# Expert blocks of 256 rows in place of 128 in a routed feed-forward kernel

## The chip, the core and the metric

One NeuronCore of a Trainium2 chip runs the whole kernel in one launch. The metric is the device time of one execution in microseconds. The core has five engines that run their own instruction lists and meet at semaphores: TensorE (PE) multiplies matrices, VectorE (DVE) and ScalarE (ACT) work on tiles, GpSimd (POOL) does small tile work and issues the indirect DMAs, SyncE (SP) issues most plain DMAs. A semaphore is a counter: one instruction raises it when it ends, another waits until it has reached a value. Matrix products land in PSUM, eight banks of 512 f32 columns on 128 partitions; everything else on the chip lies in SBUF.

## The reference

The input x has 16 sequences of 256 tokens with 128 features: 4096 rows. Three residual steps follow each other:

```
x = x + 0.5 * ffn(layernorm(x))
x = x + attn(layernorm(x))
x = x + 0.5 * ffn(layernorm(x))

def ffn(x_):                                  # x_ is [4096, 128]
    idx = argmax(x_ @ router.T)               # one of 8 experts for each row
    h_e = silu(x_ @ gate[e].T) * (x_ @ up[e].T)          # 256 wide, e = idx of the row
    y   = h_e @ down[e].T
    ys  = silu(x_ @ w_gate_s.T) * (x_ @ w_up_s.T) @ w_down_s.T    # the shared expert, for all rows
    return y + ys
```

`attn` is a circular convolution, a decayed sum over the sequence and a circular correlation; the change doesn't touch it. Everything is computed in f32.

## The kernel before

**The two expert stages.** Each `ffn` sends every row to its expert through HBM. While the rows are normalised and routed, POOL scatters them, 128 rows with one indirect DMA (line 334, 32 of them in a stage), into a buffer `dispatched` that has a region for each expert. A row takes its token number along. Behind the last row of each expert a full block of pad rows is written (`send_pads`, lines 242 to 246), so that a block that is only partly filled reads pads. The experts' rows are then cut into blocks of `P` = 128 rows. Since each expert's last block may be partly filled, there are `NB` = 32 + 7 = 39 blocks at most. The instruction list always has 39; blocks beyond those really needed repeat the last one and write their result to a part of the result buffer that nobody reads. DVE works out small tables from the routing counts: which expert each block has, where its rows begin, where its results go (`block_experts` and `tables`, lines 687 to 720).

**One block** takes these steps. SP loads its 128 rows (line 289). PE transposes them (line 882), two blocks at a time into one bank, so that features lie on partitions, and ACT copies the pair to SBUF (line 479). ACT also copies the expert's gate and up weights into a ring of four (`copy_up`, line 463), and DVE the down weights (`copy_down`, line 728). PE multiplies: four products with a 128x128 weight tile held in the array and the block's 128 columns moved past it, two for gate and two for up, all into one bank (line 893). ACT takes silu of the gate half (line 485), DVE multiplies it with the up half (line 742). PE makes the down product: two products that add up, with the hidden tile held and 128 columns of weights moved (line 901). DVE copies the 128x128 result out (line 747), and POOL scatters it to the tokens' rows of `returned` with one indirect DMA (line 363). When all 39 scatters have landed, SP loads `returned` back in token order (line 293), and the rows are added to x.

**The order on each engine is written out by hand.** PE does for step b: gate and up of block b+1 (`gate_up_block`), down of block b-1 (`down_block`), and at every second step a pair of transposes for blocks b+3 and b+4 (lines 909 to 921). ACT does for step b: silu of b+1, the weight copy of b+3, and at every second step the copy of the next transposed pair (lines 487 to 497). DVE does: result of b-1 out, multiply of b+1, weight copy of b+2 (lines 749 to 757). POOL waits for the result of b, scatters it, and computes token rows for a pair of blocks at every second step (lines 367 to 372). An instruction that waits holds back all that stands behind it on its engine. POOL's scatters wait for nothing but their results, and nobody reuses what a scatter reads within the stage.

**Around the experts** PE, ACT and DVE also work through the shared expert in parts with 512 columns (lines 816, 824, 436, 580); some parts lie before the blocks and some behind them. Before the blocks, SP and ACT write the pads, SP waits until pads and dispatched rows have landed, and loads the blocks one after the other. POOL fills the tile of pad rows once, early in the first stage (line 395), between scatters and the small steps of the norm.

Of the kernel before, what the change touches and what calls it, by code (L numbers as in the profile page):

```python
# [14 lines left out]
E = 8  # L15
# [10 lines left out]
CAP = N + P  # L26
X_LOADS = ((0, 1), (1, 2), (2, 4), (4, G))
AHEAD = 3
NB = NT + E - 1
NBL = NB + 1  # L30
BU = 8
PAIRS = NBL // 2
LOADS = NBL // BU
WR = 4
AHEAD_UP = 3
AHEAD_DOWN = 2
DUMP = N + E * P
# [19 lines left out]
def build(nc, x_in, gu_in, dn_in, router_in, bind_in, unbind_in, gate_in, decay_in, out):  # L57
# [6 lines left out]
    with ExitStack() as ctx:  # L64
# [21 lines left out]
        pads = sb("pads", [P, E, ROW])  # L86
# [56 lines left out]
        xs = sb("xs", [P, NBL, ROW])  # L143
        token = sb("token", [P, NBL], I32)
        xsT = sb("xsT", [P, 2, 2, P])
        eg = sb("eg", [P, WR, H])
        eh = sb("eh", [P, WR, H])
        wgu = sb("wgu", [P, WR, 2 * H])
        wdn = sb("wdn", [P, WR, HH * C])
        ey = sb("ey", [P, NBL, C])  # L150
# [40 lines left out]
        blk_in = [sem(f"blk_in{b}") for b in range(NBL)]  # L191
# [19 lines left out]
        def by_tile(ap):  # L211
            return ap.rearrange("p (t e) -> p t e", t=TPG)

# [21 lines left out]
        def y_of(b):  # L235

            return bank[2 + b % 2][:, 0:C]
# [4 lines left out]
        def send_pads(eng, experts):  # L242

            for e in experts:
                row = eng.value_load(pad_row[0:1, e:e + 1], min_val=0, max_val=E * CAP - P)
                eng.dma_start(dispatched[bass.ds(row, P), :], pads[:, e, :]).then_inc(pad_sent, 16)
# [8 lines left out]
        def _(sp):  # L255
# [19 lines left out]
            def block_row(b):  # L275
                return sp.value_load(tab_row[0:1, b:b + 1], min_val=0, max_val=E * CAP - P)

            sp.wait_ge(table_const, N_TABLE_CONST)
            for f in range(2):
# [11 lines left out]
                sp.wait_ge(blk_out, 16 * NB * (f + 1))  # L291
# [7 lines left out]
        def _(pool):  # L299
# [52 lines left out]
            def experts(f):  # L352
                def tokens(pair):

                    pool.wait_ge(blk_turn, f * PAIRS + pair + 1)
                    two = slice(2 * pair, 2 * pair + 2)
                    nc.gpsimd.tensor_tensor(token[:, two], xs[:, two, C].bitcast(I32), to_replica[:, two],
                                            ALU.add).then_inc(blk_tok, 1)

                def send(b):  # L360
                    pool.wait_ge(blk_tok, f * PAIRS + b // 2 + 1)
# [7 lines left out]
                for b in range(NB):  # L369
                    if b % 2 == 0 and b + 2 < NBL:  # L370
                        tokens(b // 2 + 1)
# [24 lines left out]
            nc.gpsimd.iota(pads[:, :, C:C + 1].bitcast(I32), [[P, E], [0, 1]], base=N, channel_multiplier=1,  # L396
# [9 lines left out]
        def _(act):  # L406
# [52 lines left out]
            def copy_up(b):  # L459

                if b % BU == 0:
                    digits[0] = load_digits(act, b // BU)
                nc.scalar.activation(wgu[:, b % WR, :], tile(gu, expert_of(digits[0], b)),  # L463
                                     ACT.Copy).then_inc(blk_wgu, 1)
# [11 lines left out]
            def experts(f):  # L476
                def evac_pair(pair):
                    act.wait_ge(blk_turn, f * PAIRS + pair + 1)
                    nc.scalar.activation(xsT[:, pair % 2, :, :],  # L479
                                         bank[pair % 2][:, 0:2 * P].rearrange("p (s c) -> p s c", s=2),  # L480
                                         ACT.Copy).then_inc(blk_xT, 1)

                def silu(b):
                    act.wait_ge(blk_gu, f * NB + b + 1)
                    nc.scalar.activation(eg[:, b % WR, :], bank[4 + b % WR][:, 0:H], ACT.Silu).then_inc(blk_silu, 1)  # L485

                evac_pair(0)
                silu(0)
                for b in range(NB):
                    if b + 1 < NB:  # L490
                        silu(b + 1)
                    if b == 0:
                        evac_pair(1)
# [489 lines left out]
```

## Time and profile before

| | |
|---|---|
| time of the runs | 323.37, 328.67 and 329.10 us, median 328.67 us |
| profiled execution | 329.47 us, of which 327.7 us lie between the first and the last instruction (the span) |
| busy over the span | PE 262.4 us (80%), PE weight loads 213.1 (65%), DVE 185.5 (57%), POOL 185.2 (57%), ACT 160.3 (49%) |
| mean granted TensorE clock | 0.944 of full speed |
| scatters of results (line 363) | 78 in both stages, 77.5 us busy, mean 993 ns |
| gate and up products (line 893) | 624 steps, 85.8 us busy |
| down products (line 901) | 312 steps, 48.2 us busy |
| result copies (line 747) | 78, mean 290 ns, 64.0 us of idle DVE before them |

A product of two f32 tiles shows as two matrix steps in the trace, so that a block's four gate and up products are eight steps. The ends of matrix steps are modelled, their starts are recorded: the cost of a step in a row of steps is read from one start to the next. A line of the timeline merges instructions of one kind that follow each other; in brackets stands how long the engine was idle before, and whose end was taken to have released it. "remote" there means that no instruction was found that did.

### The profile page before, as it was taken

Reading aid. Unit: us, or ns where it says so; the run is one execution under the profiler, and the core shown is the slowest. Engines: PE = TensorE matmul, PEld = TensorE weight load, DVE = VectorE, ACT = ScalarE, POOL = GpSimd, SP = SyncE. Lnnn points to the kernel's source line nnn. Section 1 sums busy time; section 2 is a strip of 40 time slices with the busy share of each in tenths; the row PEclk is TensorE's granted clock in tenths of the full one; section 3 lists DMA queues with packets and bytes.
Section 4 is the critical chain, followed back from the end, with each engine's and each line's share of the span. In section 5 each row is a group of like instructions: output and inputs, shape, how many; then the busy total and the mean of one; then the engine's idle time right before and its main releaser. Section 6 shows DMA issues by size and latency. Waiting matters only on the chain.

```text
span 327.7 us, 6436 instructions
## 1 busy us (share of the span) xinstructions
PE 262.4 (80%) x1788; PEld 213.1 (65%) x1788; DVE 185.5 (57%) x722; ACT 160.3 (49%) x374; POOL 185.2 (57%) x268
## 2 busy tenths in 40 slices
PE   0898996498988898896499889976898969989750
PEld 0566664267987798864386657753598969989430
DVE  3448551574453545538999898727644525544362
ACT  3545431035664666523699668510456545656200
POOL 4488787321656665662447888774125566576500
PEclk9999999599999999999859979995999997999996
DMA  7941111132333331119000111111323333211189
GB/s 190 370 180 43 41 50 53 34 99 61 90 91 96 97 82 34 49 41 254 5 1 25 40 37 35 34 58 57 86 67 95 87 93 91 67 41 43 40 234 279
DMA packets 34996, 28.42 MB, mean 87 GB/s; under 512 B 4784, under 2 KB 31792, under 8 KB 34704
## 3 DMA queue, kind: packets, MB, share of 16 engines
q1 hardware_dynamic: 25328, 16.06, 17.5%
q0 software_dynamic: 4544, 9.45, 8.6%
q10 hardware_dynamic: 5088, 2.50, 2.6%
q8 instruction: 14, 0.23, 0.3%
q14 instruction: 22, 0.18, 0.2%
HBM read 15.37 MB, written 12.62 MB: 85 GB/s over the span
## 4 chain that ended last, share of the span: by engine, by line
PE 42%; POOL 11%; DVE 10%; another core or an unknown queue 10%; issue 8%; ACT 6%; DMA 6%; SPq 3%; POOLq 1%; ACTq 1%; DVEq 0%
PE bank L893 21%; PE bank L901 7%; POOL dispatched L334 5%; PE bank L816 4%; DMA ey<-returned 3%; PE bank L882 2%; ACT wgu L463 2%; PE bank L841 2%; PE bank L824 2%; POOL scale_f L323 2%; DVE xres L548 2%; DVE st_f L532 2%; PE bank L802 2%; ACT xsT L479 2%
## 5 line engine op out<-in xcount | busy, mean ns | idle before, releaser
L363 POOL DMA_INDIRECT returned<-ey,token x78 | 77.5, 993 | 52.7 <-DVE ey L747 35.7
L893 PE MATMUL bank<-xsT,wgu 128*128 128x128 f32 x624 | 85.8, 281 | 14.9 <-ACT xsT L479 9.6
L893 PEld LDWEIGHTS bank<-xsT,wgu 128*128 128x128 f32 x624 | 76.7, 194 | 19.6 <-ACT xsT L479 11.7
L334 POOL DMA_INDIRECT dispatched<-xn,slot x64 | 64.2, 1003 | 26.2 <-issue 17.2
L816 PE MATMUL bank<-xnT,gu 128*128 128x512 f32 x128 | 68.1, 662 | 1.2 <-issue 0.4
L747 DVE COPY ey<-bank 128x128 f32<-128x128 f32 x78 | 22.6, 290 | 64.0 <-PE bank L901 52.3
L485 ACT ACTIVATE eg<-bank 128x256 f32<-128x256 f32 x78 | 29.9, 383 | 47.3 <-PE bank L893 42.0
L436 ACT ACTIVATE sg<-bank 128x512 f32<-128x512 f32 x32 | 19.0, 593 | 69.1 <-PE bank L816 30.0
L463 ACT ACTIVATE wgu<-gu 128x512 f32 x78 | 48.4, 625 | 3.5 <-issue 3.4
L901 PE MATMUL bank<-wdn,eh 128*128 128x128 f32 x312 | 48.2, 278 | 1.8 <-DVE eh L742 1.5
L901 PEld LDWEIGHTS bank<-wdn,eh 128*128 128x128 f32 x312 | 41.5, 194 | 2.4 <-DVE eh L742 1.9
L816 PEld LDWEIGHTS bank<-xnT,gu 128*128 128x128 f32 x128 | 24.0, 207 | 21.5 <-issue 20.5
L824 PEld LDWEIGHTS bank<-dn,hs 128*128 128x128 f32 x256 | 31.0, 196 | 10.6 <-DVE hs L580 7.0
L824 PE MATMUL bank<-dn,hs 128*128 128x128 f32 x256 | 32.4, 281 | 4.9 <-DVE hs L580 4.0
L742 DVE TENSOR_TENSOR eh<-eg,bank 128x256 f32<-128x256 f32 x78 | 32.2, 412 | 5.7 <-ACT eg L485 4.6
L412 ACT ACTIVATE xn<-xres,shift_f,scale_f 128x128 f32<-128x128 f32 x64 | 26.3, 484 | 12.5 <-POOL shift_f L327 12.5
L580 DVE TENSOR_TENSOR hs<-sg,bank 128x512 f32<-128x512 f32 x32 | 21.9, 683 | 12.5 <-ACT sg L436 9.6
L728 DVE COPY wdn<-dn 128x256 f32 x78 | 23.4, 300 | 4.1 <-issue 4.1
L841 PEld LDWEIGHTS bank<-routerT,xnT 128*128 128x128 f32 x128 | 18.3, 213 | 9.5 <-issue 7.4
L323 POOL TENSOR_TENSOR scale_f<-var_f,minus_half 128x4 f32<-128x4 f32 x16 | 16.4, 1026 | 10.0 <-DVE minus_mean_f L543 9.7
L603 DVE TENSOR_REDUCE top<-bank 128x4 f32<-128x32 f32 x16 | 3.1, 192 | 30.7 <-remote 17.1
L841 PE MATMUL bank<-routerT,xnT 128*128 128x8 f32 x128 | 17.7, 265 | 2.8 <-ACT xnT L427 1.3
(96 smaller groups left out, 290.2 us busy)
## 6 DMA issues: line engine op xcount, KB each, us to landing
xs<-dispatched SPq DMA_DIRECT2D x80, 66.0 KB, 1.9
ey<-returned SPq DMA_DIRECT2D x16, 256.0 KB, 5.1
gu<-in_gu SPq DMA_DIRECT2D x1, 2048.0 KB
out<-xres ACTq DMA_DIRECT2D x8, 256.0 KB, 5.0
returned<-ey,token POOLq DMA_INDIRECT x78
dn<-in_dn SPq DMA_DIRECT2D x1, 1024.0 KB
dispatched<-xn,slot POOLq DMA_INDIRECT x64
dispatched<-pads SPq DMA_DIRECT2D x10, 66.0 KB
```

Source lines behind the costliest of these rows:

```text
L334: nc.gpsimd.indirect_dma_start(dispatched[:, :], bass.IndirectOffsetOnAxis(slot[:, i:i + 1], 0), xn[:, i, :], None, bounds_check=last_row) ...
L363: nc.gpsimd.indirect_dma_start(returned[:, :], bass.IndirectOffsetOnAxis(token[:, b:b + 1], 0), ey[:, b, :], None, bounds_check=last_back) ...
L412: nc.scalar.activation(dst[:, at * TPG + t, 0:C], xres[:, i, :], ACT.Identity, bias=shift[kind][:, i:i + 1], scale=scale[kind][:, i:i + 1] ...
L463: nc.scalar.activation(wgu[:, b % WR, :], tile(gu, expert_of(digits[0], b)), ACT.Copy).then_inc(blk_wgu, 1)
L485: nc.scalar.activation(eg[:, b % WR, :], bank[4 + b % WR][:, 0:H], ACT.Silu).then_inc(blk_silu, 1)
L728: nc.vector.tensor_copy(wdn[:, b % WR, :], tile(dn[:].rearrange("p e h c -> p e (h c)"), expert_of(digits[0], b)))
L742: nc.vector.tensor_tensor(eh[:, b % WR, :], eg[:, b % WR, :], bank[4 + b % WR][:, H:2 * H], ALU.mult).then_inc(blk_mul, 1)
L816: last = nc.tensor.matmul(ps[:], gu[:, SHARED, at:at + P], xnT[:, g, :], start=True, stop=True)
L824: last = nc.tensor.matmul(o_ps[:, t * C:(t + 1) * C], hs[:, n % 2, h, t * P:(t + 1) * P], dn[:, SHARED, h, :], start=(h == 0), stop=(h == ...
L841: last = nc.tensor.matmul(rt[:, t * E:(t + 1) * E], xnT[:, k, t * P:(t + 1) * P], routerT[:], start=True, stop=True)
L893: last = nc.tensor.matmul(bank[4 + b % WR][:, i * P:(i + 1) * P], wgu[:, b % WR, i * P:(i + 1) * P], xsT[:, b // 2 % 2, b % 2, :], start=T ...
L901: last = nc.tensor.matmul(y_of(b), eh[:, b % WR, h * P:(h + 1) * P], wdn[:, b % WR, h * C:(h + 1) * C], start=(h == 0), stop=(h == HH - 1))
```

## The change

Blocks have 256 rows (`BW` = 2 x 128). The number of blocks in the list falls from 39 to 16 + 7 = 23, that of 128-row halves rises from 39 to 46. Partition p of a loaded block holds rows 2p and 2p+1, so that each partition's load is one run of 1056 bytes in place of 528. Gate and up have a bank each, and each of the four weight tiles meets 256 columns. Silu and multiply work on 512 columns, the result copy on 256. The down products stay 128 columns wide, and there are four for a block. Two indirect DMAs of 128 rows send a block's results. Rings of transposed rows, hidden tiles and banks have two blocks; a gate product now waits for the multiply of two blocks before (`blk_mul`). The pads of each expert are 256 rows. The main parts of the diff:

```
+SUB = 2
+BW = SUB * P
+CAP = N + BW
-NB = NT + E - 1
+NB = N // BW + E - 1
+RING = 2
...
-        pads = sb("pads", [P, E, ROW])
+        pads = sb("pads", [P, E, SUB, ROW])
...
+        def gate_of(b):
+            return bank[4 + 2 * (b % RING)]
+        def up_of(b):
+            return bank[5 + 2 * (b % RING)]
+        def block_at(row):
+            return dispatched[bass.ds(row, BW), :].rearrange("(p s) c -> p s c", s=SUB)
...
 (SP)
-                for b in range(NBL):
+                for b in range(NB):
                     row = rows[b] if b < 2 else block_row(b)
-                    sp.dma_start(xs[:, b, :], dispatched[bass.ds(row, P), :]).then_inc(blk_in[b], 16)
+                    sp.dma_start(xs[:, b, :, :], block_at(row)).then_inc(blk_in[b], 16)
...
 (POOL)
+                    pool.wait_ge(blk_tok, f * NB + b + 1)
                     pool.wait_ge(blk_y, f * NB + b + 1)
-                    nc.gpsimd.indirect_dma_start(
-                        returned[:, :], bass.IndirectOffsetOnAxis(token[:, b:b + 1], 0),
-                        ey[:, b, :], None, bounds_check=last_back).then_inc(blk_out, 16)
+                    for t in range(SUB):
+                        nc.gpsimd.indirect_dma_start(
+                            returned[:, :], bass.IndirectOffsetOnAxis(token[:, b, t:t + 1], 0),
+                            ey[:, b * SUB + t, :], None, bounds_check=last_back).then_inc(blk_out, 16)
...
 (ACT)
+                evac_rows_of(0)
+                evac_rows_of(1)
                 silu(0)
+                evac_rows_of(2)
                 for b in range(NB):
                     if b + 1 < NB:
                         silu(b + 1)
                     if b + AHEAD_UP < NB:
                         copy_up(b + AHEAD_UP)
+                        evac_rows_of(b + AHEAD_UP)
...
 (DVE)
-                    nc.vector.tensor_copy(ey[:, b, :], y_of(b)).then_inc(blk_y, 1)
+                    nc.vector.tensor_copy(ey[:, b * SUB:(b + 1) * SUB, :],
+                                          y_of(b)[:, 0:SUB * C].rearrange("p (t c) -> p t c", t=SUB)).then_inc(blk_y, 1)
...
 (PE)
+                def turn_block(b):
+                    pe.wait_ge(blk_in[b], (f + 1) * 16)
+                    for t in range(SUB):
+                        last = nc.tensor.transpose(bank[b % RING][:, t * P:(t + 1) * P], xs[:, b, t, 0:C], ident[:])
                     last.then_inc(blk_turn, 1)
...
+                    pe.wait_ge(blk_xT, f * NB + b + 1)
+                    wait_pos(pe, blk_mul, f * NB + b - RING + 1 if b >= RING else 0)
+                    for ps, at in ((gate_of(b), 0), (up_of(b), H)):
+                        for h in range(HH):
+                            last = nc.tensor.matmul(ps[:, h * BW:(h + 1) * BW],
+                                                    wgu[:, b % WR, at + h * P:at + (h + 1) * P], xsT[:, b % RING, :],
+                                                    start=True, stop=True)
                     last.then_inc(blk_gu, 1)
...
+                    for t in range(SUB):
+                        for h in range(HH):
+                            last = nc.tensor.matmul(y_of(b)[:, t * C:(t + 1) * C],
+                                                    eh[:, b % RING, h, t * P:(t + 1) * P],
+                                                    wdn[:, b % WR, h * C:(h + 1) * C],
+                                                    start=(h == 0), stop=(h == HH - 1))
                     last.then_inc(blk_dn, 1)
...
+                turn_block(1)
                 gate_up_block(0)
+                turn_block(2)
                 for b in range(NB):
                     if b + 1 < NB:
                         gate_up_block(b + 1)
+                    if b > 0:
                         down_block(b - 1)
+                    if b + AHEAD_UP < NB:
+                        turn_block(b + AHEAD_UP)
                 down_block(NB - 1)
```

## Rows read from the trace of the kernel before

**Rows 1.** Stretches, both expert stages: us, PE, PEld, DVE, ACT, POOL busy, PEclk, DMA, GB/s
```profile
74.90:145.60 70.70, 63.13 (x513) 58.80 (x514) 32.46 (x116) 39.55 (x95) 42.55 (x58) 1.00 0.26 72
237.30:310.30 73.00, 64.64 (x514) 60.27 (x515) 33.27 (x117) 39.50 (x95) 42.66 (x58) 0.98 0.25 70
```
**Rows 2.** Timeline of PE: start, length (us), line, operation, shape, count [idle before]
```profile
74.98 2.02 PE L893 MATMUL bank<-xsT,wgu 128*128 128x128 f32 x16 [0.68 <-ACT xsT L479]
...
80.75 1.06 PE L893 MATMUL bank<-xsT,wgu 128*128 128x128 f32 x8
81.64 0.61 PE L901 MATMUL bank<-wdn,eh 128*128 128x128 f32 x4
82.09 0.38 PE L882 MATMUL bank<-ident,xs 128*128 128x128 f32 x2
82.31 1.06 PE L893 MATMUL bank<-xsT,wgu 128*128 128x128 f32 x8
...
142.76 3.70 PE L816 MATMUL bank<-xnT,gu 128*128 128x512 f32 x8 [0.38 <-issue]
```
**Rows 3.** Timeline of PE, the second stage's first products
```profile
237.37 2.05 PE L893 MATMUL bank<-xsT,wgu 128*128 128x128 f32 x16 [0.98 <-DVE xres L548]
```
**Rows 4.** Timeline of POOL, result scatters of the first stage, 39 in all
```profile
80.47 1.00 POOL L363 DMA_INDIRECT returned<-ey,token  x1 [2.97 <-DVE ey L747]
...
85.97 0.97 POOL L363 DMA_INDIRECT returned<-ey,token  x1 [1.59 <-DVE ey L747]
...
87.33 1.00 POOL L363 DMA_INDIRECT returned<-ey,token  x1 [0.16 <-issue]
88.64 0.97 POOL L363 DMA_INDIRECT returned<-ey,token  x1 [0.30 <-issue]
...
91.44 1.00 POOL L363 DMA_INDIRECT returned<-ey,token  x1 [1.61 <-DVE ey L747]
...
112.46 1.00 POOL L363 DMA_INDIRECT returned<-ey,token  x1 [0.73 <-issue]
113.76 0.97 POOL L363 DMA_INDIRECT returned<-ey,token  x1 [0.30 <-issue]
...
115.66 1.00 POOL L363 DMA_INDIRECT returned<-ey,token  x1 [0.71 <-issue]
...
144.63 0.97 POOL L363 DMA_INDIRECT returned<-ey,token  x1 [0.30 <-issue]
```
**Rows 5.** Timeline of POOL, first and last of 39 scatters of the second stage
```profile
242.89 1.00 POOL L363 DMA_INDIRECT returned<-ey,token  x1 [2.97 <-DVE ey L747]
...
309.31 0.97 POOL L363 DMA_INDIRECT returned<-ey,token  x1 [0.30 <-issue]
```
**Rows 6.** Timeline of ACT, silu of two blocks in the first stage
```profile
81.84 0.39 ACT L485 ACTIVATE eg<-bank 128x256 f32<-128x256 f32 x1 [0.44 <-PE bank L893]
...
88.86 0.38 ACT L485 ACTIVATE eg<-bank 128x256 f32<-128x256 f32 x1 [1.47 <-PE bank L893]
```
**Rows 7.** Timeline of PE around 87 us
```profile
86.65 1.16 PE L893 MATMUL bank<-xsT,wgu 128*128 128x128 f32 x8
87.65 0.61 PE L901 MATMUL bank<-wdn,eh 128*128 128x128 f32 x4
```
**Rows 8.** Timeline of DVE, a result copy
```profile
90.39 0.29 DVE L747 COPY ey<-bank 128x128 f32<-128x128 f32 x1 [2.37 <-PE bank L901]
```
**Rows 9.** Timeline of all engines around 270 us, second stage
```profile
267.87 1.00 POOL L363 DMA_INDIRECT returned<-ey,token  x1 [0.16 <-issue]
...
269.78 0.38 ACT L485 ACTIVATE eg<-bank 128x256 f32<-128x256 f32 x1 [3.28 <-remote]
...
270.73 2.08 PE L893 MATMUL bank<-xsT,wgu 128*128 128x128 f32 x8 [2.36 <-ACT wgu L463]
```
**Rows 10.** Timeline of POOL, the pad tile is filled
```profile
21.55 0.98 POOL L395 MEMSET pads<- 128x1056 f32 x1
```
**Rows 11.** Chain of waits ahead of the first stage: pads landing, after SP's last issue
```profile
69.77 1.65 DMA dispatched<-pads
```

More of the change, by code:

```diff
@@ L190, in build @@
         selfed, x2_done = sem("selfed"), sem("x2_done")
-        blk_in = [sem(f"blk_in{b}") for b in range(NBL)]
+        blk_in = [sem(f"blk_in{b}") for b in range(NB)]
         blk_out = sem("blk_out")
@@ L244, in send_pads @@
             for e in experts:
-                row = eng.value_load(pad_row[0:1, e:e + 1], min_val=0, max_val=E * CAP - P)
-                eng.dma_start(dispatched[bass.ds(row, P), :], pads[:, e, :]).then_inc(pad_sent, 16)
+                row = eng.value_load(pad_row[0:1, e:e + 1], min_val=0, max_val=E * CAP - BW)
+                eng.dma_start(block_at(row), pads[:, e, :, :]).then_inc(pad_sent, 16)
         def wait_pos(eng, s, value):
@@ L369, in experts @@
                 for b in range(NB):
-                    if b % 2 == 0 and b + 2 < NBL:
-                        tokens(b // 2 + 1)
+                    if b + 1 < NB:
+                        tokens(b + 1)
                     send(b)
@@ L877, in experts @@
             def experts(f):
-                def turn_pair(pair):
-                    for t in range(2):
-                        pe.wait_ge(blk_in[2 * pair + t], (f + 1) * 16)
-                        last = nc.tensor.transpose(bank[pair % 2][:, t * P:(t + 1) * P], xs[:, 2 * pair + t, 0:C],
-                                                   ident[:])
+                def turn_block(b):
+                    pe.wait_ge(blk_in[b], (f + 1) * 16)
+                    for t in range(SUB):
+                        last = nc.tensor.transpose(bank[b % RING][:, t * P:(t + 1) * P], xs[:, b, t, 0:C], ident[:])
@@ L884, in turn_pair @@
                     last.then_inc(blk_turn, 1)
                 def gate_up_block(b):
-                    if b % 2 == 0:
-                        pe.wait_ge(blk_xT, f * PAIRS + b // 2 + 1)
-                    if b % 2 or b < AHEAD_UP:
-                        pe.wait_ge(blk_wgu, f * NB + b + 1)
-                    for i in range(2 * HH):
-                        last = nc.tensor.matmul(bank[4 + b % WR][:, i * P:(i + 1) * P],
-                                                wgu[:, b % WR, i * P:(i + 1) * P], xsT[:, b // 2 % 2, b % 2, :],
-                                                start=True, stop=True)
+                    pe.wait_ge(blk_xT, f * NB + b + 1)
@@ L896, in gate_up_block @@
                     last.then_inc(blk_gu, 1)
                 def down_block(b):
-                    pe.wait_ge(blk_mul, f * NB + b + 1)
-                    for h in range(HH):
-                        last = nc.tensor.matmul(y_of(b), eh[:, b % WR, h * P:(h + 1) * P],
-                                                wdn[:, b % WR, h * C:(h + 1) * C],
-                                                start=(h == 0), stop=(h == HH - 1))
+                    if b + RING >= NB:
+                        pe.wait_ge(blk_mul, f * NB + b + 1)
```

74 lines of the change are left out of this document (32 added, 42 removed).

## The prediction

> **What bounds the kernel now.** I read the stretches first. Each expert stage, from its first product to the end of its last scatter, takes 70.6 us (74.98 to 144.63 + 0.97) and 72.9 us (237.37 to 309.31 + 0.97) [rows 1 to 5]; together that is 44% of the span, and nearly all of the change lies in it. PE is busy 63 of 71 us, at the full clock level in the first stage and 0.98 of it in the second; DVE and ACT are busy for about half [rows 1]. So it looks bound by PE.
>
> The timeline of PE says how much of that is needed. In an unbroken run the eight steps of a block's gate and up products start at 80.75 and the down steps at 81.64: 0.89 us, or 0.111 us a step. The transposes follow 0.45 us later, and a pair of them costs 0.22 us (82.09 to 82.31) [rows 2]. Thirty-nine blocks need 39 x (0.89 + 0.45) + 20 x 0.22 = 56.7 us. The stage takes 14 to 16 us more.
>
> The timeline of POOL shows what goes with the rest. The 39 scatters run from 80.47 to 145.60, 65.1 us, and in the second stage from 242.89 to 310.28, 67.4 us [rows 4, 5]: 1.67 and 1.73 us each, though one follows another after only 1.31 us (87.33 to 88.64) or, with a token step between, 1.36 us (85.97 to 87.33). They come in bursts: three from 85.97, the last ending at 89.61, then 1.83 us of nothing until 91.44 [rows 4]. What ends the pause is a result copy of DVE, which had waited 2.37 us for a down product and started at 90.39 [rows 8].
>
> That wait is the core of my reading. Where POOL had not yet scattered in a burst, silu starts at 81.84, 0.03 us behind the gate step's end at 81.81 [rows 2, 6]. In the burst, gate and up end at 87.81 and silu starts at 88.86, 1.05 us late; the down product behind them ends at 88.26 and its copy starts at 90.39, 2.1 us late and 0.8 us after the burst's end [rows 4, 6 to 8]. PE's starts show no gap there. So from about the second scatter of a burst on, **news of finished PE work reaches ACT and DVE late**, until POOL pauses. POOL pauses only when it lacks results, which is when DVE hasn't heard of a down product: the stage swings between the two. A longer burst holds longer: after one whose last scatter starts at 267.87, ACT had waited 3.28 us when it starts again at 269.78, PE has stood 2.36 us, and its next products take 2.08 us in place of 1.16 [rows 7, 9]: the lower of the clock's two levels, 1.2 GHz for 2.4.
>
> **The change, part by part** (for each stage, against 329.47 us for the profiled execution, 327.7 of it span; this execution is 0.8 us above the median).
>
> *PE.* A step of 512 columns costs (3.70 - 0.66) / 7 = 0.43 us from start to start, 0.66 being one step's own mean length, 3.9 times the 128-column one [rows 2]. A 256-column step is not in the trace: at least 0.111 us, at most two of 128, 0.223. On the line between the two widths it is 0.219, and I take that. Gate and up of a block: 8 x 0.219 = 1.75 us; four down products 0.89; two transposes 0.22; sum 2.86 us, for 23 blocks 65.8 us. That is 9 us **more** than before: 46 halves in place of 39, and little saved by wider steps.
>
> *ACT and DVE.* Fewer and longer instructions, 23 of a kind for 39. Their half-idle rows [rows 1] leave room for 46/39 of the columns; I cost this at nothing. If the cover were gone, the added columns would show, at most 7/39 of their busy time: 6 us of DVE, 7 of ACT. The result copy is the exception: it stands between a down product and POOL. One of 128 columns takes 0.29 us [rows 8], one of 256 between 0.29 and 0.58; I take 0.43, the middle.
>
> *Until the first scatter.* Before, 5.49 us from the first product (74.98 to 80.47) [rows 2, 4] and 5.52 in the second stage [rows 3, 5]. After: three gate and up groups, two turns and a down group, 3 x 1.75 + 2 x 0.22 + 0.89 = 6.58, the copy 0.43, and 0.76 for POOL to begin (the copy from 90.39 ends at 90.68, the scatter starts at 91.44 [rows 4, 8]): 7.77 us, **+2.26**.
>
> *The scatters.* Forty-six. Bounds: unbroken, POOL needs 2.67 us for two, 46/2 x 2.67 = 61.3 us, less than before; PE's 2.86 for a block gives nearly the same end. At the other end, bursts of one block: 1.31 + 0.97, then the pause of 1.83 + 0.14 for the longer copy, 4.25 us a block, 96 us. Between them, bursts of two blocks: 1.31 + 1.36 + 1.31 + 0.97 + 1.97 = 6.92, 3.46 a block. The nearest row is a burst of two scatters as it stands in the trace: 112.46, 113.76, then 115.66, **3.20 us for two** [rows 4]. I take that: three-scatter bursts by the sum give 5.47 / 3 = 1.82, and the stages average only 1.70, so sums of bursts come out some 7% high, and 3.46 less 7% is 3.2 too. 22 x 3.20 + 2.28 = 72.7 us, against 66.3 on average: **+6.4**.
>
> *The new waits.* Gate and up of block b+1 wait for the multiply of b-1; behind them on PE stand down b-1 and the turn of b+3, and ACT's copy of those rows waits for that turn. From the last news that ACT had, PE has down, turn, gate and up, down, turn to do: 0.89 + 0.22 + 1.75 + 0.89 + 0.22 = 3.97 us, about twice what it had (0.45 + 0.22 + 0.89 + 0.45 = 2.01). That shelters PE from a hold of 3 us, but not POOL, which still gets no results in it. So I add nothing here.
>
> *Ahead of the stage.* POOL's fill of the pads doubles, 0.98 us more [rows 10], with scatters queued behind it on POOL that run without a break: +1.0, once. Pads are twice the bytes; the last of them lands 1.65 us after its issue [rows 11], between nothing and another 1.65 more: +0.5 a stage. The first loads are longer too, in part under DVE's own end in the second stage [rows 3]; left in that 0.5. SP's queue gets 23 loads in place of 40. The tables on DVE get shorter; pads are later than tables, so nothing.
>
> *Sum.* 2 x (2.26 + 6.4 + 0.5) + 1.0 = 19.3 us: 348.8 us for the profiled execution, **348 us** for the median, slower by 5.9%.
>
> **Rivals.**
>
> *The holds go with something that the change cuts.* The loads of blocks share the stage with the scatters, and become fewer with longer runs; if the late news comes of them, PE's order sets the end: 65.8 less the two turns ahead of the first product 0.43, then 0.43 + 0.76 + 2.28, 68.8 us from first product to last scatter, against 71.8. 2 x (-3.0 + 0.5) + 1.0 = -4.0: about 325 us, not slower. For it: PE's doubled lead. Against it: the timing follows POOL's bursts, and POOL has only 2.86 - 2.67 = 0.19 us a block to make up pauses. It decides if pauses after bursts fall under some 0.2 us.
>
> *Holds grow with the longer burst.* Bursts of two blocks are the rule at 3.46: 22 x 3.46 + 2.28 = 78.4, 2 x (2.26 + 12.1 + 0.5) + 1.0 = +30.7: 359 us. For it: the longer burst with its stop and lower clock [rows 9]. Against: the 7%.
>
> *Weights set the step, not columns.* Then a 256-column step costs little more than 0.111 us, say 0.135: gate and up 1.08, a block 2.19 us, and POOL alone bounds the stage. First scatter after 3 x 1.08 + 2 x 0.22 + 0.89 + 0.43 + 0.76 = 5.76, +0.25; run 61.3 to 72.7; 320 to 343 us, 331 in the middle. Against it: 512 columns cost 3.9 times 128 [rows 2]. The Trainium skill (TensorE: Matmul & The Clock Gate, section Back-to-back issue gap) speaks for it: in a stream of weight loads and products a product of 128 columns comes every 81 ns and one of 512 every 131 ns, 1.6 times for four times the columns. By that rule an estimate for 256 columns is 1.2 times a 128-column step, which gives the 331 us; the trace disagrees, with 0.43 to 0.111.
>
> **How the numbers follow.** A measurement of this kernel can tell about 2%, 322 to 335 us. My forecast has 0.54 (340 to 353 us), longer holds 0.20 (353 to 364), holds gone 0.21 (321 to 332), weights 0.05. Slower by over 2%: 0.54 + 0.20 = 0.74, and 0.01 of the weights' upper end, 0.75. Faster: a fifth of the holds gone and of the weights, 0.05. Same: the rest of these two, 0.20. The range of 8 in 10 takes the forecast whole, most of either neighbour: 325 to 359; the likeliest case alone has 340 to 353.
>
> **What would show it.** Right: products of 256 columns starting 0.22 us apart; 7.8 us to the first scatter; scatters in pairs or fours with pauses of nearly 2 us behind them, result copies that wait for down products long ended, 46 in about 73 us; PE with idle stretches though it has more work. Wrong: a PE without gaps for 65 us with POOL close behind it (holds gone), steps of 0.14 us (weights), or a POOL that never pauses.

## The result

The 256-row kernel takes **346.42 us** in the median (341.92 to 351.69 us) where the 128-row kernel takes 328.71 us on the same chip: a ratio of **1.053, with a 95% interval of 1.037 to 1.070**. The ratio compares fast executions alone; the profiled one of the 256-row kernel, 1.6% above the fastest, is not among them. Forecast were 348 us, in a range of 325 to 359. The profiled execution took 347.23 us, with a span of 345.5 us, 17.8 us more than before.

### The profile after

From the page, the costliest groups of the blocks (columns: line, engine, operation, tiles, shape, count | busy us, mean ns of one | idle time of the engine before them):

```profile
L379 POOL DMA_INDIRECT returned<-ey,token x92 | 90.9, 988 | 58.9 <-DVE ey L761 35.5
L907 PE MATMUL bank<-xsT,wgu 128*128 128x256 f32 x368 | 87.9, 382 | 7.7 <-DVE eh L756 7.3
...
L761 DVE COPY ey<-bank 128x256 f32<-128x256 f32 x46 | 19.5, 423 | 85.6 <-PE bank L917 68.4
L917 PE MATMUL bank<-wdn,eh 128*128 128x128 f32 x368 | 49.3, 279 | 6.7 <-DVE eh L756 6.7
```

Ahead of 46 result copies DVE stood idle for 68.4 us until a down product of PE was done, though those products had often ended long before, as will be seen. The two expert stages as stretches (us, PE, PEld, DVE, ACT, POOL busy, PEclk, DMA, GB/s):

```profile
74.40:154.10 79.70, 72.58 (x420) 63.34 (x420) 28.47 (x68) 32.14 (x66) 49.91 (x68) 0.96 0.25 73
248.00:328.50 80.50, 72.25 (x428) 63.18 (x427) 28.35 (x68) 32.72 (x67) 49.79 (x68) 0.98 0.24 71
```

Beside [rows 1], PE is busy for 9.5 and 7.6 us more in a stage, and the stage is 9.0 and 7.5 us longer. (2.2 and 1.9 us of what PE does more are products of the shared expert that fall into these stretches, 5.03 and 5.40 us for 2.84 and 3.49.) Of the 17.8 us of span, +16.6 lie in the two stages from the first product to the end of the last scatter (79.7 and 80.4 us, before 70.6 and 72.9 [rows 2 to 5]), -0.6 ahead of the first stage, +2.1 between the stages and -0.3 behind the second.

PE's timeline, around 288 us:

```profile
285.82 1.89 PE L907 MATMUL bank<-xsT,wgu 128*128 128x256 f32 x8
287.55 1.05 PE L917 MATMUL bank<-wdn,eh 128*128 128x128 f32 x8
288.44 0.38 PE L896 MATMUL bank<-ident,xs 128*128 128x128 f32 x2
288.66 1.89 PE L907 MATMUL bank<-xsT,wgu 128*128 128x256 f32 x8
290.38 1.05 PE L917 MATMUL bank<-wdn,eh 128*128 128x128 f32 x8
```

From one group of eight steps to the down products are 1.73 us, so a 256-column step costs 0.216 us, and a block 2.84 us in an unbroken run (285.82 to 288.66). POOL's scatters in the same stretch, and what ACT and DVE do then:

```profile
282.93 1.00 POOL L379 DMA_INDIRECT returned<-ey,token  x1 [2.19 <-DVE ey L761]
284.23 0.97 POOL L379 DMA_INDIRECT returned<-ey,token  x1 [0.30 <-issue]
...
292.22 0.97 POOL L379 DMA_INDIRECT returned<-ey,token  x1 [0.30 <-issue]
...
295.66 1.00 POOL L379 DMA_INDIRECT returned<-ey,token  x1 [2.24 <-DVE ey L761]
```

```profile
287.75 0.60 ACT L500 ACTIVATE eg<-bank 128x512 f32<-128x512 f32 x1 [1.34 <-PE bank L907]
...
290.10 0.39 ACT L496 ACTIVATE xsT<-bank 128x256 f32<-128x256 f32 x1 [1.24 <-PE bank L896]
292.97 0.60 ACT L500 ACTIVATE eg<-bank 128x512 f32<-128x512 f32 x1 [2.48 <-remote]
```

```profile
289.37 0.43 DVE L761 COPY ey<-bank 128x256 f32<-128x256 f32 x1 [2.35 <-PE bank L917]
...
294.47 0.42 DVE L761 COPY ey<-bank 128x256 f32<-128x256 f32 x1 [3.82 <-PE bank L917]
```

Eight scatters go out from 282.93 to 293.19, then POOL stands for 2.2 us beside a token step, 12.7 us for four blocks. (Bursts of eight are the rule from about 120 us in the first stage and 270 us in the second; before that most are shorter.) The lateness grows through the burst: the silu of 287.75 starts 0.04 us behind its products (end 287.71); the result copy of 289.37 is 0.8 us behind its down product (288.60), the row copy of 290.10 is 1.3 us behind its turn (288.82), the silu of 292.97 2.4 us behind 290.55, and the result copy of 294.47 3.0 us behind a down product that ended at 291.43. It is the pattern of [rows 4, 6 to 9] with a longer period, and it goes on long after SP's last block load, issued at 96.6 us in the first stage. At its end PE loses 1.1 us once in a cycle, and at the end of the first stage more:

```profile
146.47 2.07 PE L917 MATMUL bank<-wdn,eh 128*128 128x128 f32 x8 [3.38 <-DVE eh L756]
149.07 5.19 PE L831 MATMUL bank<-xnT,gu 128*128 128x512 f32 x8 [0.52 <-issue]
```

After standing for 3.38 us PE takes 2.07 us for the last down products, 1.05 elsewhere: the clock's lower level, 1.2 GHz for 2.4, and 5.19 us for the eight steps of the shared expert that took 3.70 before [rows 2].

### The profile page after: what moved, and what is told of

It is laid out like the page before. It is cut to its first block, busy times and chain, and to the rows that moved or that the text cites. A ratio compares the mean times of both kernels' runs of the same rounds, so it can differ in the third digit from the quotient of the medians.

```text
span 345.5 us, 5524 instructions
## 1 busy us (share of the span) xinstructions
PE 286.1 (83%) x1600; PEld 225.1 (65%) x1600; DVE 175.6 (51%) x626; ACT 145.6 (42%) x316; POOL 200.2 (58%) x288
## 3 DMA queue, kind: packets, MB, share of 16 engines
q0 software_dynamic: 4992, 10.36, 9.0%
## 4 chain that ended last, share of the span: by engine, by line
PE 49%; DVE 12%; another core or an unknown queue 9%; issue 9%; POOL 8%; DMA 6%; SPq 2%; ACT 2%; DVEq 1%; POOLq 0%; ACTq 0%
PE bank L907 21%; PE bank L917 10%; PE bank L831 7%; POOL dispatched L349 3%; PE bank L856 3%; DMA ey<-returned 3%; PE bank L839 3%; PE bank L896 2%; PE bank L817 2%; DVE eh L756 2%; POOL returned L379 2%; POOL scale_f L338 1%; DVE st_f L546 1%; DVE xres L562 1%
## 5 line engine op out<-in xcount | busy, mean ns | idle before, releaser
L379 POOL DMA_INDIRECT returned<-ey,token x92 | 90.9, 988 | 58.9 <-DVE ey L761 35.5
L907 PE MATMUL bank<-xsT,wgu 128*128 128x256 f32 x368 | 87.9, 382 | 7.7 <-DVE eh L756 7.3
L907 PEld LDWEIGHTS bank<-xsT,wgu 128*128 128x128 f32 x368 | 66.3, 190 | 16.9 <-ACT xsT L496 9.2
L761 DVE COPY ey<-bank 128x256 f32<-128x256 f32 x46 | 19.5, 423 | 85.6 <-PE bank L917 68.4
L917 PEld LDWEIGHTS bank<-wdn,eh 128*128 128x128 f32 x368 | 48.6, 194 | 9.2 <-DVE eh L756 7.0
L500 ACT ACTIVATE eg<-bank 128x512 f32<-128x512 f32 x46 | 27.4, 596 | 58.2 <-PE bank L907 36.1
L756 DVE TENSOR_TENSOR eh<-eg,bank 128x512 f32<-128x512 f32 x46 | 31.2, 679 | 9.4 <-ACT eg L500 9.3
L594 DVE TENSOR_TENSOR hs<-sg,bank 128x512 f32<-128x512 f32 x32 | 21.8, 682 | 16.6 <-ACT sg L452 15.4
L479 ACT ACTIVATE wgu<-gu 128x512 f32 x46 | 28.3, 624 | 1.0 <-issue 0.8
L496 ACT ACTIVATE xsT<-bank 128x256 f32<-128x256 f32 x46 | 17.6, 383 | 19.3 <-remote 9.8
L896 PE MATMUL bank<-ident,xs 128*128 128x128 f32 x92 | 17.7, 274 | 2.5 <-DMA xs<-dispatched 1.6
```

Source lines behind the costliest of these rows:

```text
L379: nc.gpsimd.indirect_dma_start(returned[:, :], bass.IndirectOffsetOnAxis(token[:, b, t:t + 1], 0), ey[:, b * SUB + t, :], None, bounds_che ...
L479: copied = nc.scalar.activation(wgu[:, b % WR, :], tile(gu, expert_of(digits[0], b)), ACT.Copy)
L500: nc.scalar.activation(eg[:, b % RING, :, :], by_half(gate_of(b)), ACT.Silu).then_inc(blk_silu, 1)
L756: nc.vector.tensor_tensor(eh[:, b % RING, :, :], eg[:, b % RING, :, :], by_half(up_of(b)), ALU.mult).then_inc(blk_mul, 1)
L896: last = nc.tensor.transpose(bank[b % RING][:, t * P:(t + 1) * P], xs[:, b, t, 0:C], ident[:])
L907: last = nc.tensor.matmul(ps[:, h * BW:(h + 1) * BW], wgu[:, b % WR, at + h * P:at + (h + 1) * P], xsT[:, b % RING, :], start=True, stop=True)
```

## The experiments

Three theories stood. **Holds**: POOL's result scatters, close upon each other, keep the news of finished PE work from ACT and DVE. **PE's work**: the order of PE, 7 halves longer, is what the time follows, and the holds are a side show. **Memory**: loads and written rows, not POOL, make the news late. "The stretch" is the time from the first gate product to the end of the last down product; it is 67.4 and 69.0 us in the 128-row kernel and 74.1 and 74.0 in the 256-row one, for the two stages.

### No scatter before the last result

```
                 tokens(0)
+                for b in range(1, NB):
+                    tokens(b)
+                pool.wait_ge(blk_y, (f + 1) * NB)
                 for b in range(NB):
                     send(b)
```

> The 256-row kernel, in which POOL first computes all tokens and issues the stage's 46 result scatters only when the last result lies in SBUF. The stage gets longer for that, since all scatters follow the work; what counts is the stretch from the first gate product to the end of the last down product (74.1 and 73.9 us in the 256-row kernel). Holds (news of finished PE work is late while POOL scatters): no hold is left, silu starts within 0.1 us of each gate and up group, result copies stop waiting for long-ended down products, PE runs without gaps, 23 x 2.84 less two turns plus about 2 us for the last hidden tile = 66 to 67.5 us. Rival, loads of blocks or another load on memory make the news late: the waits stay and the stretch stays at 72 to 75 us. Rival, ACT or DVE are too slow for 256-row blocks: PE's gaps stay, 72 to 75 us.

The stretch was 67.3 and 65.5 us. PE ran without one gap between its first and its last blocks, and ACT right behind it:

```profile
99.17 0.60 ACT L501 ACTIVATE eg<-bank 128x512 f32<-128x512 f32 x1 [1.34 <-PE bank L908]
...
102.00 0.60 ACT L501 ACTIVATE eg<-bank 128x512 f32<-128x512 f32 x1 [1.34 <-PE bank L908]
104.84 0.60 ACT L501 ACTIVATE eg<-bank 128x512 f32<-128x512 f32 x1 [1.34 <-PE bank L908]
```

A silu every 2.84 us, which is PE's own pace. ACT and DVE are quick enough for 256-row blocks, and the order has no stall of its own. (The extra 1.8 us of the first stage are mostly its first group, at the lower clock level: 3.14 us for 1.89.) The run as a whole, 438.86 us, pays for the 46 scatters behind each stage.

### One scatter in a block

```
-                def send(b):
+                def send(b, halves=(0,)):
...
-                    for t in range(SUB):
+                    for t in halves:
...
+                for b in range(NB):
+                    send(b, (1,))
```

> The 256-row kernel, in which the first half of each block is scattered as before, 23 scatters in the stage, and the 23 second halves only behind the last block. Holds: with one scatter of about 1 us in 2.9 us POOL is idle between any two, so that news comes on time; first gate product to last down product in 66 to 69 us, PE with few gaps. If a single scatter already holds the news back for 1 us or more: 69 to 73 us. If the holds don't come of POOL's scatters: 74 us, as it is.

67.3 and 65.5 us, the same as with none. A scatter alone holds nothing back:

```profile
96.69 1.00 POOL L379 DMA_INDIRECT returned<-ey,token  x1 [1.61 <-DVE ey L763]
97.72 0.20 POOL L371 TENSOR_TENSOR token<-xs,to_replica 128x2 int32<-128x2 int32 x1
99.53 0.99 POOL L379 DMA_INDIRECT returned<-ey,token  x1 [1.61 <-DVE ey L763]
```

```profile
97.45 0.60 ACT L502 ACTIVATE eg<-bank 128x512 f32<-128x512 f32 x1 [1.35 <-PE bank L909]
```

The products before this silu ended at 97.41 (95.52 + 1.89), in the middle of a scatter, and it starts at 97.45.

### The same bytes, sent otherwise

By SP, eight blocks late (for POOL only the tokens are left):

```
+                    if b >= 8:
+                        sp.wait_ge(blk_y, f * NB + b - 7)
+                        for t in range(SUB):
+                            at = ((b - 8) * SUB + t) * P
+                            sp.dma_start(returned[at:at + P, :], ey[:, (b - 8) * SUB + t, :]).then_inc(blk_out, 16)
```

> The 256-row kernel, in which SP sends each result half of 128 rows by a plain transfer of the same bytes, eight blocks late, to rows in block order (the rows are not put back to their tokens: that part is left out), and POOL only computes tokens. It tells what in a scatter makes the news late. If it is POOL's own work on the transfer: no holds, 66 to 68 us from the first gate product to the last down product, and the run as a whole 325 to 335 us. If it is the writing of 128 rows to memory: holds stay, 72 to 75 us.

By POOL, at once:

```
-                        nc.gpsimd.indirect_dma_start(
-                            returned[:, :], bass.IndirectOffsetOnAxis(token[:, b, t:t + 1], 0),
-                            ey[:, b * SUB + t, :], None, bounds_check=last_back).then_inc(blk_out, 16)
+                        at = (b * SUB + t) * P
+                        nc.gpsimd.dma_start(returned[at:at + P, :], ey[:, b * SUB + t, :]).then_inc(blk_out, 16)
```

> The 256-row kernel, in which POOL sends each result half of 128 rows by a plain transfer to rows in block order in place of an indirect one (the rows are not put back to their tokens). If it is the work of building indirect transfers on POOL that holds the news back: no holds, 66 to 68 us from the first gate product to the last down product. If any transfer that POOL issues does it: holds stay, 70 to 75 us.

SP: 67.3 and 65.5 us, the run 323.73 us. POOL: 65.6 and 65.5 us, the run 323.93 us, beside 334.49 us of the 128-row kernel on that chip. The stages of the second one:

```profile
74.10:142.00 67.90, 67.17 (x416) 61.02 (x415) 27.91 (x67) 32.24 (x66) 29.70 (x68) 1.00 0.28 85
235.30:303.10 67.80, 67.06 (x416) 60.98 (x415) 27.81 (x67) 32.23 (x65) 29.56 (x68) 1.00 0.29 85
```

PE is busy for all of it, at the full clock level, with the same loads and the same written bytes, and more of them in a second (85 GB/s for 73). POOL's queue moves as many packets and bytes as with indirect transfers (4992 packets, 10.36 MB in the whole run). So neither the loads nor the writing of these bytes makes the news late, and the memory theory falls. One difference is left: the plain transfers write rows that follow each other, the indirect ones rows all over `returned`. No run sends indirect transfers to rows in order, so that the two aren't told apart.

### The same on the 128-row kernel

```
-                    nc.gpsimd.indirect_dma_start(
...
+                    nc.gpsimd.dma_start(returned[b * P:(b + 1) * P, :], ey[:, b, :]).then_inc(blk_out, 16)
```

> The 128-row kernel, in which POOL sends each block's results by a plain transfer to rows in block order (rows are not put back to their tokens), the partner of the same edit on the 256-row kernel, 323.9 us with 65.6 us from the first gate product to the last down product. It gives what the change costs without any holds. Theory: PE needs 56.7 us and a tail of about 1 us, 57 to 59 us for the stretch, 305 to 310 us as a whole, so that the change costs 14 to 19 us by PE's work alone, and holds cost the 128-row kernel 9 to 11 us a stage, the 256-row one 7 to 8. If the 128-row order had stalls of its own that the scatters hide: 60 to 67 us.

```profile
75.20:134.70 59.50, 58.29 (x509) 57.22 (x510) 32.12 (x115) 39.20 (x94) 25.23 (x58) 1.00 0.31 86
225.60:285.10 59.50, 58.23 (x508) 57.15 (x509) 32.13 (x115) 39.12 (x94) 25.01 (x58) 1.00 0.31 85
```

The stretch is 58.0 and 58.2 us and the run 304.87 us. So **without holds in the expert stages the change costs 19.1 us** (323.93 - 304.87, one execution of each, on two chips whose 128-row kernels differ by 0.2 us), with them 17.7. The holds cost the 128-row kernel 9.4 and 10.8 us a stage, the 256-row one 8.5 and 8.5. What the change adds is PE's longer order, 7.6 and 7.3 us a stage; of holds it has rather less.

The result scatters aren't the only ones. Ahead of the experts POOL sends the dispatch by the same kind of transfer, and there the trace of the kernel before shows the longest lateness of all. Twelve scatters go out 1.28 to 1.36 us apart, from 43.46 to 58.59:

```profile
57.62 0.97 POOL L334 DMA_INDIRECT dispatched<-xn,slot  x1 [0.30 <-issue]
63.24 0.97 POOL L334 DMA_INDIRECT dispatched<-xn,slot  x1 [4.64 <-DVE slot L622]
```

```profile
52.40 1.03 PE L841 MATMUL bank<-routerT,xnT 128*128 128x8 f32 x8 [0.99 <-issue]
53.29 1.96 PE L816 MATMUL bank<-xnT,gu 128*128 128x512 f32 x4
62.10 0.19 PE L874 MATMUL bank<-chosen,ones 128*128 128x8 bf16 x1 [6.85 <-DVE chosen L609]
```

```profile
60.70 0.19 DVE L603 TENSOR_REDUCE top<-bank 128x4 f32<-128x32 f32 x1 [7.63 <-remote]
60.76 0.60 ACT L436 ACTIVATE sg<-bank 128x512 f32<-128x512 f32 x1 [10.68 <-remote]
```

DVE starts its reduce 7.3 us behind the router's products (end 53.43), ACT its silu 5.5 us behind the gate products (55.25), both some 2.1 us after POOL's burst has ended, and PE stands for 6.85 us. In the second stage it is 5.5 us after eight scatters (217.59 to 223.08). The change doesn't touch these scatters, and they are in the two kernels with plain result transfers as well; no experiment spaced them.

### POOL busy with something else

The plain transfers by POOL, and behind each a fill of an idle tile:

```
+        idle = sb("idle", [P, 8, 700])
...
+                        nc.gpsimd.memset(idle[:, (b * SUB + t) % 8, :], 0.0)
```

> The 256-row kernel with plain transfers by POOL (rows not put back to their tokens) and a fill of an idle tile of about 0.7 us behind each, so that POOL is as long at work for a block as with two indirect scatters, about 2.6 to 2.8 us of 2.84. If POOL being busy without a pause is what makes news late: holds are back, 70 to 76 us from the first gate product to the last down product. If it is the indirect transfer itself: PE runs without gaps, 65.5 to 67.5 us.

```profile
102.54 0.56 POOL L381 DMA_DIRECT2D returned<-ey  x1 [0.29 <-POOL token L372]
103.09 0.70 POOL L382 MEMSET idle<- 128x700 f32 x1
103.71 0.54 POOL L381 DMA_DIRECT2D returned<-ey  x1
104.24 0.70 POOL L382 MEMSET idle<- 128x700 f32 x1
104.89 0.20 POOL L372 TENSOR_TENSOR token<-xs,to_replica 128x2 int32<-128x2 int32 x1
```

POOL is at work for 2.55 of 2.84 us, and the stretch is 67.3 and 65.6 us, with a silu every 2.84 us. (The run, 335.81 us, is longer than with plain transfers alone because the stages, counted from their first product, end 4.8 and 3.9 us later with POOL now as slow as PE, and because the first stage began 4.7 us later, behind work that is the same in both.) A busy POOL holds nothing back, nor does a plain transfer that it issues. Indirect transfers close upon each other do.

### The wide step undone

```
-                            last = nc.tensor.matmul(ps[:, h * BW:(h + 1) * BW],
-                                                    wgu[:, b % WR, at + h * P:at + (h + 1) * P], xsT[:, b % RING, :],
-                                                    start=True, stop=True)
+                            for t in range(SUB):
+                                last = nc.tensor.matmul(ps[:, h * BW + t * P:h * BW + (t + 1) * P],
+                                                        wgu[:, b % WR, at + h * P:at + (h + 1) * P],
+                                                        xsT[:, b % RING, t * P:(t + 1) * P], start=True, stop=True)
```

> The 256-row kernel, in which each gate and up weight tile meets two products of 128 columns in place of one of 256: the wide step alone is undone. If a step costs by its columns: 16 steps of 0.111 us in place of 8 of 0.216, 1.78 us for 1.73 in a block, at most 1 us a stage, 346 to 348 us, same as the 256-row kernel. If a weight tile's load had set the step, the wide step would save and undoing it cost 8 x 0.1 x 23 x 2 = 30 us or more. Rival on the holds: if the late news piles up with the number of products PE finishes, 26 in place of 18 for a block bring the burst of eight scatters down to four or so and the stage to 80 us: 355 to 365 us.

359.95 us, 1.075 times the 128-row kernel (1.068 to 1.083), against 1.053 (1.037 to 1.070) for the 256-row kernel; the two were not run beside each other. Sixteen steps take 1.78 us (105.55 to 107.33), 0.05 more than eight wide ones, 1.2 us a stage: the step costs by its columns. But the stages are 84.0 and 83.0 us to the last scatter, 4.3 and 2.6 more, and the bursts are shorter (of the 13.0 us more of span another 4.1 lie ahead of the first stage, in work that is the same: POOL's last four dispatch scatters begin at 66.19 in place of 62.29, and the mean granted clock up to there is 0.89 for 0.95):

```profile
102.60 0.99 POOL L379 DMA_INDIRECT returned<-ey,token  x1 [1.81 <-DVE ey L761]
...
109.28 0.97 POOL L379 DMA_INDIRECT returned<-ey,token  x1 [0.30 <-issue]
...
112.59 0.99 POOL L379 DMA_INDIRECT returned<-ey,token  x1 [2.11 <-DVE ey L761]
```

Six scatters in 10.0 us, 3.33 us a block for 3.18. My theory had "no change" here and missed. The rival's time came in (355 to 365 us), with 4.1 us of it from ahead of the stages, but not its bursts of four or its stage of 80 us. The wide product seems to help (the two intervals just touch), but not by the step: with fewer and longer products POOL gets on for longer until it has to pause. That lateness has to do with the number of products is what this suggests; it is not shown, since nothing else about the products was varied. The number alone can't be it: a burst goes with 72 matrix steps of PE here (four blocks of 18) and 78 with the wide step undone (three of 26), but with 39 in the 128-row kernel (three of 13).

### Room between the scatters

The 128-row kernel, with a fill of an idle tile of 300 columns behind each result scatter:

```
+        idle = sb("idle", [P, 8, 300])
...
                         ey[:, b, :], None, bounds_check=last_back).then_inc(blk_out, 16)
+                    nc.gpsimd.memset(idle[:, b % 8, :], 0.0)
```

> The 128-row kernel, in which POOL fills an idle tile for some 0.3 us after each result scatter, so that scatters are no less than about 1.5 to 1.65 us apart and never back to back. If news is late only when scatters follow each other at 1.3 us: no holds, the scatters follow at 1.5 to 1.65 us, 59 to 64 us for 39 against 65 and 67 now, 315 to 326 us. If late news piles up with POOL's share of time in scatters, whatever the spacing, and drains only in a real pause: pauses stay, every burst is longer by the fills, 39 scatters in 66 to 76 us, 328 to 345 us, same or slower.

325.98 us against 334.26, **0.978 (0.971 to 0.984)**: POOL does 29.3 us more work, and the kernel is faster.

```profile
98.60 0.98 POOL L364 DMA_INDIRECT returned<-ey,token  x1 [0.17 <-issue]
99.58 0.39 POOL L367 MEMSET idle<- 128x300 f32 x1
99.95 0.18 POOL L358 TENSOR_TENSOR token<-xs,to_replica 128x2 int32<-128x2 int32 x1
100.29 1.01 POOL L364 DMA_INDIRECT returned<-ey,token  x1 [0.16 <-POOL token L358]
101.30 0.36 POOL L367 MEMSET idle<- 128x300 f32 x1
101.83 0.98 POOL L364 DMA_INDIRECT returned<-ey,token  x1 [0.17 <-issue]
```

In the first stage POOL never pauses for a result again, and in the second once, for 2.05 us: 0.53 to 0.80 us lie between two scatters in place of 0.30 to 0.39, and the 39 take 62.3 and 63.7 us for 65.1 and 67.4. The stretch falls to 60.9 and 59.2 us; the last scatter now ends 6.9 and 10.0 us behind the last down product, 3.2 and 3.9 before.

Half the fill (150 columns, 0.25 us) on both kernels:

```
+        idle = sb("idle", [P, 8, 150])
...
                         for the 256-row kernel
+                        nc.gpsimd.memset(idle[:, (b * SUB + t) % 8, :], 0.0)
...
                         for the 128-row kernel
+                    nc.gpsimd.memset(idle[:, b % 8, :], 0.0)
```

> The 256-row kernel, in which POOL fills an idle tile for some 0.25 us after each result scatter, so that the engine has 0.42 us or more between scatters in place of 0.30 and a pair takes 2.94 us. If a slightly wider gap is enough for the news to get through, as 0.55 us was in the 128-row kernel: no pauses, 22 x 2.94 + 2.4 = 67 us for 46 scatters in place of 72, the run 8 to 11 us shorter than the 256-row kernel, 1.02 to 1.03 times the 128-row kernel. If 0.42 us is too narrow: bursts and pauses stay, 72 to 76 us for the scatters, 1.05 to 1.08 times the 128-row kernel.

> The 128-row kernel with fills of 0.25 us in place of 0.375, so that scatters are 1.41 and, with a token step, 1.53 us apart, 1.47 on average, about what PE needs for a block (1.45). If the gap of 0.42 us lets the news through: 39 scatters in 57 to 59 us, 0.95 to 0.965 times the 128-row kernel, the fastest so far. If it is too narrow: bursts and pauses are back, 62 to 68 us, 0.98 to 1.01 times.

The 256-row kernel came to 342.91 us, 1.042 (1.031 to 1.052) times the 128-row one: 46 scatters in 69.0 and 69.6 us, few pauses, the stretch 69.9 and 70.7. By the two ratios that is some 4 us less than the 256-row kernel takes, where 8 to 11 were expected, and as the intervals of the two overlap (1.037 to 1.070 without fills), a gain isn't shown: the scatters took 2.7 and 2.9 us less, but in the first stage they began 9.7 us after the first product, with a first group at the lower clock level (3.10 us). In the 128-row kernel the room is too narrow: 0.990 (0.985 to 0.995), 65.2 and 64.7 us, at first with a pause after every fourth scatter:

```profile
86.33 1.01 POOL L364 DMA_INDIRECT returned<-ey,token  x1 [1.14 <-DVE ey L749]
...
90.82 0.98 POOL L364 DMA_INDIRECT returned<-ey,token  x1 [0.17 <-issue]
...
93.31 1.01 POOL L364 DMA_INDIRECT returned<-ey,token  x1 [1.13 <-DVE ey L749]
```

Then two fills of unequal length, so that the room is the same with and without a token step:

```
+                    nc.gpsimd.memset(idle[:, b % 8, 0:100 if b % 2 else 300], 0.0)
```

> The 128-row kernel with the fill of 0.375 us where no token step follows and one of about 0.2 us where one does, so that every scatter starts about 1.54 us after the last and each gap is 0.54 us. If the gap decides, as the fill of 0.375 us gave no pauses: 39 scatters in 59 to 60 us in place of 62.3 and 63.7, some 2 to 3 us a stage less than with the even fills, 0.96 to 0.975 times the 128-row kernel. If two fills of 0.375 us worked by the longer gap at the token step alone (0.69 us): pauses are back, 0.98 to 1.0 times.

and with less room:

```
+                    nc.gpsimd.memset(idle[:, b % 8, 0:40 if b % 2 else 220], 0.0)
```

> The same with fills of about 0.3 and 0.15 us: a scatter every 1.48 us, gaps of 0.48 us, between the 0.42 us that left pauses after every fourth scatter in the 128-row kernel and the 0.55 us that left none. If news gets through: 57 to 58 us for 39 scatters, 0.95 to 0.97 times the 128-row kernel. If it piles up slowly: pauses of about 1 us more after six to ten scatters, 59 to 62 us, 0.97 to 0.985 times.

Both missed the full gain. The wider gave 323.52 us, 0.983 (0.977 to 0.988): pauses came back after five or six scatters (the last 18 and 20 of the stages ran without), 62.9 and 63.7 us for all, no better than with equal fills. The narrower gave 327.83 us, 0.992 (0.987 to 0.997), 62.7 and 64.4 us. So there is no sharp width. In the 128-row kernel, the more room between two scatters on average, the more of them go out until a pause early in a stage: three at 0.35 us [rows 4] and at 0.46 (40 and 220 columns), four at 0.50 (150), five or six at 0.53 (100 and 300), no pause in the first stage at 0.62 (300). Room bought this way costs POOL much of what it saves in pauses. Of the kernels that put the rows back to their tokens, the one with fills of 300 columns has the best ratio, though its interval overlaps that of 100 and 300 columns, and it beats both kernels of the change.

## Why the prediction was right

**PE's steps**: 0.219 forecast, 0.216 measured; 2.86 for a block, 2.84 measured. (The 0.66 us in the step's sum is the mean length of line 816's steps on the page, 662 ns; [rows 2] don't show it.) The Trainium skill (TensorE: Matmul & The Clock Gate, section Back-to-back issue gap), from whose figures for a stream of products an estimate for 256 columns is 1.2 times a 128-column step, differs from the trace here: 0.216 to 0.111 us, 1.9 times. The rival built on it falls.

**First scatter**: 7.77 us after the first product, measured 8.02 (74.41 to 82.43) and 7.92. The result copy: 0.43, measured 0.42.

**The run of scatters**: 72.7 us, measured 71.7 and 72.5; 3.20 us a block, measured 3.18. The size is right, but the row that I took it from, a burst of two with a pause of 0.93 us that no result copy ends [rows 4], isn't what happens: the rule is eight scatters at 1.33 us and a pause of 2.2. Sums of bursts of one or two blocks (96 and 78.4 us) were too high because I let the lateness begin with the second scatter, as it does in the 128-row kernel; here it begins with the fifth or sixth. That a short burst with a short pause has the pace of a long one with a long pause is luck: two errors cancelled.

**What the cost is made of**: I put the 9 us of PE's longer order aside and booked the cost to the scatters (+6.4) and the late start (+2.3). With plain transfers there are no holds in these stages, and the change costs 7.6 and 7.3 us a stage between first gate and last down product all the same. Put together with the holds: PE's order +7.6 and +7.3, holds -0.9 and -2.4, and from the last down product to the last scatter's end +2.3 and +2.6; the sum, 9.0 and 7.5, is what the stages got longer (9.1 and 7.5). The holds set the pace of both kernels, but the difference is PE's seven halves more.

**Ahead of the stages**: +2.0 in all. The fill of the pads did grow, by 0.88 us (0.98 to 1.86 [rows 10]), but the first stage began 0.6 us earlier. The step that failed is "scatters queued behind it that run without a break": towards the end of the dispatch POOL stood for 4.64 us in the 128-row kernel until DVE had slots, and for 2.13 and 0.93 us in the 256-row one, so that nearly a microsecond early on cost nothing. From the first of the last four dispatch scatters to the stage's first product are 0.38 and 0.55 us more in the two stages (11.74 to 12.12 and 11.74 to 12.29), my 0.5. The other 1.6 us between the stages I did not follow up.

**Rivals**: "holds go" (325 us, not slower) needs the loads to be the cause; the holds stayed after the last load. As a price of a stage it was good: 68.8 us from first product to last scatter, and 67.7 and 67.6 with POOL's plain transfers. "Holds grow with the burst" (359 us) had a burst of two blocks at 6.92 us; four blocks in 12.7 us were cheaper, because a pause costs about the same however many scatters stand before it (in the second stage, token step included, 2.1 us after three, 2.0 after five, 2.3 to 2.5 after eight).

**What stays open** is how indirect transfers of POOL delay what ACT and DVE hear of PE, and whether their form or their scattered rows do it. The Trainium skill (Trainium Architecture — The Big Picture, section What this means for kernel authors) has engines independent unless a semaphore ties them, with DVE and GpSimd's shared port as the one place where engines contend on their side of SBUF. It doesn't say how soon a raised semaphore is heard. By it that port alone can't be the cause, since ACT was 2.4 us late at 292.97 as well.

## To carry to other kernels

When an engine "waits" for a product that ended long ago, look for what another engine does in that time, and for whether the lateness ends when that one pauses; an experiment that only moves that work away prices the whole effect. Price a coarser tile first by the work that its padding adds to the busiest engine (46 halves for 39): here that was paid however the stalls fell. Indirect transfers of 128 rows from POOL may be better given some room between them than sent back to back, if their reader is not waiting: it gained 2.2% in the 128-row kernel, and nothing clear of noise in the 256-row one.

## What was not expected of the hardware

- Back-to-back indirect scatters by POOL (1.28 to 1.36 us apart) make the end of PE's work known to ACT and DVE up to 3.0 us late, growing through the burst, and 7.3 us late after twelve in the dispatch; one in 2.84 us doesn't, nor do plain transfers of the same bytes (0.55 us of POOL each), alone or with fills that keep POOL at work for 2.55 of 2.84 us.
- A fill of 0.375 us on POOL behind each result scatter, work that nothing uses, made the 128-row kernel 2.2% faster (1.6 to 2.9).
- How long a burst lasts until POOL has to pause differs with the kernel at the same spacing: mostly three scatters with 128-row blocks, eight with 256-row ones, six when the latter's products were cut in two. What sets it isn't shown.
